# Stacking the queries by DMA from the sync queue instead of by selection products, with eight key buffers

## The reference, cut to what matters

```python
q = shape(H @ Wq, Lq) * dph ** (-0.5)        # H = layernorm(x), 16 heads of dph = 8
k = shape(T @ Wk, Lkv)                       # T = ctx_1024, 64 keys a batch
v = shape(T @ Wv, Lkv)
scores = jnp.einsum('bhqd,bhkd->bhqk', q, k) + ext        # ext masks keys
attn = jax.nn.softmax(scores.astype(jnp.float32), axis=-1)
x = x + jnp.einsum('bhqk,bhkd->bhqd', attn, v).transpose(0, 2, 1, 3).reshape(B, Lq, INNER) @ Wo
x = x + moe(layernorm(x))     # top 2 of 8 experts, a capacity per expert, silu(gate) * up, then wo
```

## Time and profile before

| what | value |
|---|---|
| median of 3 runs | 417.09 us (416.58 to 418.83) |
| the profiled execution | 418.15 us |
| its span, first to last instruction | 416.3 us |
| around the span | 1.85 us |
| mean granted clock of TensorE | 0.946 of full speed |
| busy over the span | PE 87%, DVE 63%, POOL 55%, ACT 46% |

### The profile page before, as it was taken

One profiled execution on the slowest core, in us unless ns is written; L12 is line 12 of the kernel. 1 busy time (PEld: TensorE's weight loads), 2 busy tenths in 40 slices (PEclk: granted clock), 3 DMA queues, 4 the chain that ended last, 5 costly groups with the idle time before them and its releaser, 6 DMA issues.

```text
span 416.3 us, 8894 instructions
## 1 busy us (share of the span) xinstructions
PE 360.4 (87%) x3012; PEld 311.7 (75%) x3012; DVE 260.7 (63%) x893; ACT 189.4 (46%) x430; POOL 228.9 (55%) x190
## 2 busy tenths in 40 slices
PE   0768889999899998849599999999999999999980
PEld 0456666677667665436599998999989899998980
DVE  4956888988998988762155455555554646455430
ACT  2444656667667765421233343434434444343320
POOL 9514231045437667777036566474764738557564
PEclk9986899999999999668699999999999999999996
DMA  8998011122223221111503724537363463723222
GB/s 246 262 308 291 3 21 31 30 46 67 41 47 90 64 81 56 65 58 54 136 9 32 168 27 73 114 33 168 27 119 73 35 156 32 157 35 34 26 27 25
DMA packets 41958, 35.05 MB, mean 84 GB/s; under 512 B 9136, under 2 KB 38320, under 8 KB 41776
## 3 DMA queue, kind: packets, MB, share of 16 engines
q1 hardware_dynamic: 27824, 24.72, 21.3%
q0 software_dynamic: 13568, 9.58, 17.0%
q10 hardware_dynamic: 528, 0.27, 0.2%
HBM read 21.64 MB, written 17.73 MB: 95 GB/s over the span
## 4 chain that ended last, share of the span: by engine, by line
PE 51%; DVE 19%; POOL 11%; issue 8%; DMA 6%; ACT 3%; POOLq 1%; DVEq 0%; ACTq 0%
PE bank L823 13%; PE bank L629 7%; PE bank L631 6%; POOL slots L443 6%; PE bank L630 6%; POOL out L477 4%; DMA out<-ys,idx 4%; PE bank L706 3%; DVE mneg L924 2%; PE bank L658 2%; PE bank L685 2%; DVE rall L1043 2%; PE bank L672 2%; PE bank L686 1%; PE bank L793 1%
## 5 line engine op out<-in xcount | busy, mean ns | idle before, releaser
L477 POOL DMA_INDIRECT out<-ys,idx x80 | 125.1, 1564 | 87.7 <-DVE ys L1122 36.9
L1148 DVE TENSOR_TENSOR h<-sg,bank 128x256 f32<-128x256 f32 x160 | 66.2, 418 | 77.4 <-ACT sg L614 70.2
L614 ACT ACTIVATE sg<-bank 128x256 f32<-128x256 f32 x160 | 61.5, 385 | 102.6 <-PE bank L631 96.2
L629 PE MATMUL bank<-ex_hi,w_hi 128*128 128x256 f32 x320 | 94.1, 294 | 4.1 <-DVE h L1148 4.1
L631 PE MATMUL bank<-ex_lo,w_hi 128*128 128x256 f32 x320 | 89.6, 280 | 0.0
L630 PE MATMUL bank<-ex_hi,w_lo 128*128 128x256 f32 x320 | 89.5, 280 | 0.0
L823 PE MATMUL bank<-w_raw,h 128*128 128x128 f32 x640 | 78.7, 276 | 1.7 <-DVE h L1148 1.4
L823 PEld LDWEIGHTS bank<-w_raw,h 128*128 128x128 f32 x640 | 74.7, 191 | 3.6 <-DVE h L1148 1.9
L443 POOL DMA_INDIRECT slots<-rall,slot x64 | 64.4, 1007 | 19.6 <-issue 15.5
L629 PEld LDWEIGHTS bank<-ex_hi,w_hi 128*128 128x128 f32 x320 | 61.1, 191 | 5.6 <-DVE h L1148 5.5
L630 PEld LDWEIGHTS bank<-ex_hi,w_lo 128*128 128x128 f32 x320 | 61.2, 191 | 0.0
(11 more groups left out here) (120 smaller groups left out, 540.2 us busy)
## 6 DMA issues: line engine op xcount, KB each, us to landing
slots<-in_empty SPq DMA_DIRECT2D x8, 660.0 KB, 11.0
xl<-slots SPq DMA_DIRECT2D x7, 660.0 KB, 6.7
w_raw<-in_wgu SPq DMA_DIRECT2D x8, 512.0 KB, 3.6
X<-in_x SPq DMA_DIRECT2D x4, 512.0 KB, 8.1
w_raw<-in_wdn SPq DMA_DIRECT2D x8, 256.0 KB, 4.0
out<-X SPq DMA_DIRECT2D x16, 128.0 KB
out<-ys,idx POOLq DMA_INDIRECT x80, 3.3
ks<-kc SPq DMA_DIRECT2D x72, 16.0 KB
```

The source lines that it names most:

```text
L477: nc.gpsimd.indirect_dma_start(out=out[:, :], out_offset=bass.IndirectOffsetOnAxis(ap=IDX[v][:, j:j + 1], axis=0), in_=YS[c][:, t, :], in_ ...
L614: nc.scalar.activation(SG[m % 2][:], GATE_PS[m % 2][:, 0:2 * P], ACT.Silu).then_inc(sg_ready, 1)
L629: nc.tensor.matmul(ps, hi, m_hi, start=True, stop=False)
L1148: nc.vector.tensor_tensor(H[n % 2][:, f, :], SG[m % 2][:], UP_PS[m % 2][:, 0:2 * P], ALU.mult).then_inc(h_ready, 1)
```

## The change

The queries of a batch are stacked by three DMAs on SP, one for each of the high, low, high parts; the eight products, their two copies and the selection matrices go. The columns of `Wq` are reordered on the host so that one DMA can write 32 rows and four groups from the 128 rows of `Q_HI` or `Q_LO`. There are eight key buffers: POOL spreads the keys of batches 0 to 7, and SP places those of batches 8 to 15 four batches at a time, a quarter of their rows in each of four steps. To make room, three arrays of the set-up share memory with arrays of the steps.

```diff
-KBUF = 4
+KBUF = 8
@@ set-up arrays
-        CTXM = s1("ctxm", [P, B, LK])
-        CTX_HI = s1("ctx_hi", [P, B * LK], F32R)
-        CTX_LO = s1("ctx_lo", [P, B * LK], F32R)
-        MASKI = s1("maski", [P, B, LK], I32)
-        SEL_HI = s1("sel_hi", [P, GROUPS, 3, 32], F32R)
-        SEL_LO = s1("sel_lo", [P, GROUPS, 3, 32], F32R)
+        CTX_HI, CTX_LO = [KS[:, 4 + n].rearrange("p g n -> p (g n)") for n in range(2)]
+        CTXM = PROBS[0][:, 0:2].rearrange("p g s q -> p (g s q)").rearrange("p (b k) -> p b k", k=LK)
+        MASKI = PROBS[1][:, 0:2].rearrange("p g s q -> p (g s q)").bitcast(I32)
@@ sync, after the fills, the weights, and its waits for k_used and ext_in
-            def place_keys(j):
-                b = slice(2 * j, 2 * j + 2)
-                to = slice(2 * j % KBUF, 2 * j % KBUF + 2)
-                done = keys_in[j % 2]
-                sp.wait_ge(st_full, 4 * (2 * j - 2))
-                for part in range(4):
-                    for h in range(HG):
-                        rows = slice(32 * part + DPH * h, 32 * part + DPH * h + DPH) if part < 3 else slice(ONE_ROW, ONE_ROW + 1)
-                        sp.dma_start(KS[rows, to, :, h * LK:(h + 1) * LK].bitcast(F32), KC[rows, b, :, :]).then_inc(done, 16)
+            def stack_queries(i):
+
+                sp.wait_ge(qlo_ready, i + 1)
+                if i >= 2:
+                    sp.wait_ge(st_full, 4 * (i - 1))
+                for part, q in enumerate((Q_HI, Q_LO, Q_HI)):
+                    sp.dma_start(QS[i % 2][32 * part:32 * part + 32, :, :].bitcast(F32),
+                                 q[:].bitcast(F32)).then_inc(qs_in[i % 2], 16)
+
+            def place_keys(i):
+
+                j, n = i // 4, i % 4
+                b, to = slice(4 * j, 4 * j + 4), slice(4 * j % KBUF, 4 * j % KBUF + 4)
+                done = keys_in[j % 2]
+                if n == 0:
+                    sp.wait_ge(st_full, 4 * (4 * j - 4))
+                for h in range(HG):
+                    rows = slice(32 * n + DPH * h, 32 * n + DPH * h + DPH) if n < 3 else slice(ONE_ROW, ONE_ROW + 1)
+                    sp.dma_start(KS[rows, to, :, h * LK:(h + 1) * LK].bitcast(F32), KC[rows, b, :, :]).then_inc(done, 16)
-            for j in range(2, B // 2):
-                place_keys(j)
-                store_sums(2 * j - 4)
-                store_sums(2 * j - 3)
-            for i in range(B - 4, B):
+            for i in range(B):
+                stack_queries(i)
+                if 5 <= i < 13:
+                    place_keys(i + 3)
+                if i >= 3:
+                    store_sums(i - 3)
+            for i in range(B - 3, B):
                 store_sums(i)
@@ gpsimd: the memsets and three copies that fill SEL_HI and SEL_LO are taken out
@@ scalar
-            def stack_queries(it, off, h):
-
-                i, u = 2 * it + off, off % 2
-                act.wait_ge(sel_full, 2 * i + (3 + h))
-                if h == 0:
-                    wait(act, st_full, 4 * i)
-                nc.scalar.copy(QS[1 - u][0:96, 2 * h:2 * h + 2, :].rearrange("p g q -> p (g q)"), QP[0:96, :]).then_inc(qs_ready, 1)
@@ scalar, step
                 if has(it, off, 1):
                     act.wait_ge(q_full, i + 2)
+                    wait(act, qs_in[u], 48 * ((i + 2) // 2))
                     nc.scalar.mul(Q_HI[:], M0[:, 0:LQ], SCALE).then_inc(qhi_ready, 1)
-                if has(it, off, 1):
-                    stack_queries(it, off, 0)
                     act.wait_ge(mt_full, i + 1)
+                    wait(act, st_full, 4 * (i - 1))
-                if has(it, off, 1):
-                    stack_queries(it, off, 1)
@@ tensor
                 if m == 0:
-                    pe.wait_ge(qs_ready, 2 * i + 2)
+                    pe.wait_ge(qs_in[u], 48 * (i // 2 + 1))
                     if i < KBUF:
                         pe.wait_ge(ks_ready, i + 1)
                     else:
-                        pe.wait_ge(keys_in[i // 2 % 2], PLACED * (i // 4))
+                        pe.wait_ge(keys_in[i // 4 % 2], PLACED)
-            def select(it, off, h):
-                i = 2 * it + off
-                if h == 0:
-                    pe.wait_ge(qlo_ready, i + 2)
-                wait(pe, qs_ready, 2 * i + (2 + h))
-                for gg in range(2):
-                    g = 2 * h + gg
-                    ps = QP[0:96, gg * LQ:(gg + 1) * LQ]
-                    nc.tensor.matmul(ps, SEL_HI[:, g].rearrange("p a c -> p (a c)"), Q_HI[:], start=True, stop=False)
-                    mm = nc.tensor.matmul(ps, SEL_LO[:, g].rearrange("p a c -> p (a c)"), Q_LO[:], start=False, stop=True)
-                mm.then_inc(sel_full, 1)
@@ tensor, step: both calls of select are taken out (between TX2 and the values; between the logits and L793)
@@ vector, step
-                    wait(dve, sel_full, 2 * i + 2)
+                    wait(dve, qs_in[u], 48 * ((i + 2) // 2))
@@ host
-        "wq": a["L0_xattn_Wq"],
+        "wq": np.ascontiguousarray(a["L0_xattn_Wq"].reshape(D, GROUPS, 32).transpose(0, 2, 1).reshape(D, D)),
```

More of the change, by code:

```diff
@@ L219, in program @@
         q_full, qhi_ready, qlo_ready = sem("q_full"), sem("qhi_ready"), sem("qlo_ready")
-        sel_full, qs_ready = sem("sel_full"), sem("qs_ready")
+        qs_in = [sem(f"qs_in{v}") for v in range(2)]
         ks_ready, v2_clear = sem("ks_ready"), sem("v2_clear")
@@ L299, in _ @@
         def _(sp):
-            sp.dma_start(MASKI[:].rearrange("p b k -> p (b k)"),
+            sp.dma_start(MASKI,
                          mask.rearrange("b k -> (b k)").rearrange("(a n) -> a n", a=1).to_broadcast([P, B * LK])
@@ L387, in _ @@
                 nc.gpsimd.memset(MNEG[v][:], 1.0)
-            nc.gpsimd.memset(RALL[:, :, D:ROW], 0.0)
+            nc.gpsimd.memset(RALL[:, :, D:ROW], 0.0).then_inc(pool_setup, 1)
             nc.gpsimd.memset(V2[:], 0.0).then_inc(v2_clear, 1)
-            nc.gpsimd.memset(SEL_HI[:, :, 1, :].bitcast(F32), 0.0)
-            nc.gpsimd.memset(SEL_LO[:].bitcast(F32), 0.0).then_inc(pool_setup, 1)
             pool.wait_ge(pool_setup, 3)
             pool.wait_ge(const_in, 16)
[L395 to L398, removed]
             nc.gpsimd.tensor_copy(TRI[:], C[:, C_TRI:C_TRI + P])
@@ L491, in _ @@
             act.wait_ge(setup, 3)
-            nc.scalar.copy(CTX_HI[:], CTXM[:].rearrange("p b k -> p (b k)")).then_inc(ctx_split, 1)
+            nc.scalar.copy(CTX_HI, CTXM.rearrange("p b k -> p (b k)")).then_inc(ctx_split, 1)
             for n in range(8):
@@ L642, in _ @@
             pe.wait_ge(k_used, 8)
-            pe.wait_ge(pool_setup, 5)
+            pe.wait_ge(pool_setup, 4)
             def row_scores(it, off, m):
@@ L767, in step @@
                     rank(ROUTED[off])
-                if has(it, off, 1):
-                    select(it, off, 0)
                 if has(it, off, -1):
@@ L784, in step @@
                     mm.then_inc(lg_full, 1)
-                if has(it, off, 1):
-                    select(it, off, 1)
                 if has(it, off, -1):
@@ L861, in _ @@
             dve.wait_ge(mask_in, 16)
-            nc.vector.tensor_copy(MASKF[:], MASKI[:]).then_inc(setup, 1)
+            nc.vector.tensor_copy(MASKF[:], MASKI.rearrange("p (b k) -> p b k", k=LK)).then_inc(setup, 1)
             dve.wait_ge(setup, 1)
@@ L868, in _ @@
             any_b = ANY[:].unsqueeze(2).to_broadcast([P, B, LK])
-            nc.vector.tensor_tensor(CTXM[:], CTX[:], any_b, ALU.mult).then_inc(setup, 1)
+            nc.vector.tensor_tensor(CTXM, CTX[:], any_b, ALU.mult).then_inc(setup, 1)
             dve.wait_ge(wsplit, 1)
@@ L872, in _ @@
             dve.wait_ge(ctx_split, 1)
-            nc.vector.tensor_tensor(CTX_LO[:], CTXM[:].rearrange("p b k -> p (b k)"), CTX_HI[:].bitcast(F32), ALU.subtract
+            nc.vector.tensor_tensor(CTX_LO, CTXM.rearrange("p b k -> p (b k)"), CTX_HI.bitcast(F32), ALU.subtract
                                     ).then_inc(ctx_split, 1)
@@ L903, in _ @@
                 nc.vector.tensor_tensor(lo.bitcast(F32R), K_PS[n % 4][64:96, :].rearrange("p (b k) -> p b k", k=LK), lo, ALU.subtract).then_inc(k_used, 1)
-            dve.wait_ge(pool_setup, 5)
+            dve.wait_ge(pool_setup, 4)
             def norm(i, v):
```

## The result

The changed kernel takes 439.37 us (median of 4 runs, 436.71 to 439.75) against 417.96 us of the kernel before in the same job (416.58 to 420.37): a ratio of 1.0487, interval 1.0451 to 1.0523. The forecast was 432.4 us. The measured time lies in the range from 421 to 441 that was stated for it together with its rivals, but above the forecast's own range of 427 to 438. The profiled span is 437.4 us, 21.1 more.

The account below looks back on a forecast made before the run. DVE was taken to set the pace in the steps. Start 11.7, first steps -1.2, later steps -0.8, spreadings 3.4, keys 2.2 make 15.3 us more: 432.4 us, own range 427 to 438, with rivals 421 to 441.

Parts of the forecast that it names:

- The first stack: Start: batch 0's stack lands behind fills and weights in SP's queue, row scores 11.7 us late.
- The first rival: Start: the stack is not held by the fills and lands at 33.0, 0.4 late; 421.1 us, chance 0.09.
- The spreadings: Steps 3 to 6: four more key spreadings on POOL hold up DVE's RALL, 3.4 us in all.
- The last quarter of the keys: Batches 8 and 12: the last key copies land after the row scores could start; 1.1 us each, 2.2 together.
- The first steps: Steps 0 and 1, at low clock: dropped products save PE time, 1.2 us gained.
- The later steps: Seven undisturbed steps at full clock: each gains about 0.11 us, 0.8 us together.
- The later stacks: Each later step: a stack takes 4.0 us from Q_LO, covered by 4.6 to 4.7 us of step; no cost.
- The second rival: All steps: every stack is late, 5.3 us or more from Q_LO; 438.4 us, chance 0.12.
- The sum: Whole kernel: all terms together add 15.3 us, giving 432.4 us.
- a clock below full speed in the steps: Steps: sign of a wrong prediction, if with PE less busy it shows as longer projections on DVE's path.
- the fourth rival: POOL's sends: they run at their own pace from an earlier start and swallow the delay; 417 us, chance 0.03.

Follow-up runs that it names:

- experiment 1: Changed kernel with the stacks of batches 0 and 1 issued from ACT's queue instead of SP's: 440.19 us, 1.0523 to the kernel before.
- experiment 2: Changed kernel with slot fills, zeros and expert weights issued on SP behind later stacks: 428.07 us, 1.0212 to the kernel before.
- Experiment 5: Changed kernel with POOL's key spreadings moved early, four ahead of batch 0 and four in its first step: 436.09 us, 1.0388.
- Experiment 6: Kernel before with only the eight key buffers, their spreadings and quarters added; selecting products and copies kept: 422.97 us, 1.0102.
- experiment 3: Changed kernel with SP issuing each quarter of the keys ahead of the stack of its turn: 436.66 us, 1.0426.
- experiment 4: Changed kernel with products of no use on PE ahead of the row scores of batches 0, 8 and 12: 435.57 us, 1.0426.
- experiment 9: Changed kernel with fills and weights later, Q_HI copies first, non-waiting key quarters ahead of stacks, spreadings one, four, three: 420.70 us, 1.0061.

## Why the prediction was right, and where it was off

**The first stack: right in size (11.1 against 11.7), its mechanism too narrow.** The prediction had it that "the queue delivers in about the order of issue". The changed kernel fits that: the stack lands about with the last weights. But experiment 1 takes the stack out of that queue and gains only 1.6 us; experiment 2 takes away the bulk transfers and gains nearly all. The load on the engines is enough to hold it, and moving it to another queue is no cure. The first rival, which priced a stack that isn't held, got its lateness about right for a start without fills (34.19 against 33.0).

**The spreadings: right.** Steps 3 to 6 slip by 3.05 us; forecast were 3.4 less 0.33 for three quicker steps. RALL took 1.59, 1.58, 1.12 and 1.59 us. Experiment 5 gives 3.8 back over steps 2 to 6. Experiment 6 loses 4.07 in steps 3 to 6, but its clock was at 0.50 from 52 to 62 us, into step 3.

**The last quarter of the keys: mis-sized.** Forecast 2.2 us, measured 6.1 (3.24 and 2.89). The wait was somewhat above its forecast of 1.1 each, 1.6 and 1.8 us (the gains of experiment 3 less those of experiment 4), within the bounds. But the step priced a wait of PE at its own length. Behind it the granted clock stood at 0.50 for over 5 us, and that cost 1.6 and 1.1 us more.

**The first steps: of the wrong sign.** Forecast -1.2 us, measured +1.7. The saved products were costed at a low clock that was taken to be the same in both kernels. From the first row scores to X of step 2 it was 0.65 in the mean, against 0.81 before, and at 0.88 in experiment 4 the stretch took 1.6 us less. The other 1.3 us aren't settled: in experiment 4 the two steps take 27.35 us, no less than the 27.23 before, though at a higher clock, so the saving itself doesn't show there.

**The later steps: right.** Undisturbed ones take 7.83 us in place of 7.94 (step 7), the 0.11 forecast. Eight products and two copies a step were worth that much. Steps 9 to 11 won another 0.12 us. Steps 13 to 16 lost 1.07, of which 0.74 was made up by the last send; neither is explained.

**The later stacks: right.** From issue to landing 3.2 us as the median of the 28 later copies of `Q_HI`, and PE's waits for a stack, in 32 to 190 (total us, times, longest):

```profile
qs<-q_hi SPq DMA_DIRECT2D x28, 128.0 KB, 3.2
```

```profile
PE bank L651 <- DMA qs<-q_hi: 14.2, 2, 13.9
```

Nearly all of it is the first. One of the others, its last issue and the row scores that use it:

```profile
77.59 0.60 SPq L332 DMA_DIRECT2D qs<-q_hi  x1
```

```profile
81.83 0.48 PE L651 MATMUL bank<-ks,qs 97*128 97x256 f32 x2
```

`Q_LO` ended at 76.30, so the stack, 3.2 us after that issue, is there 4.5 us later, and the row scores start 5.5 later: hidden. In a step without a spreading the cover is 4.7, with little to spare. The second rival falls with it. Its 438.4 us came nearer to the measured time than the forecast's 432.4, but by luck: behind the first, PE's waits for a stack came to 0.3 us in all.

**The sum.** 11.1 + 1.7 + 3.05 + 6.1 and small change make 22.1 us at the last send, of which 21.1 reach the end; the forecast's 15.3 lacked 3.9 at the keys and 2.9 at the first steps. Of these, 2.8 and 1.6 went when experiment 4 raised the clock. The forecast had no term for that; it named a clock below full speed in the steps among the signs that it is wrong, and this sign appeared. That the delay reaches the end, against the fourth rival, is seen in the sends.

No version beat the kernel before. The best, experiment 9, is 0.6% slower, with its steps as long as before; what it loses, it loses ahead of X of step 1.

## What to carry to other kernels

Price a wait of TensorE by the wait and by the slower stretch behind it: at batches 8 and 12 waits of 1.6 and 1.8 us cost 3.2 and 2.9. Here a small DMA that the path needs was late while bulk transfers ran, whichever queue issued it; look at moving the bulk, not the small one. When work is removed from engines that don't set the pace, its gain is only what the pace-setting engine waited for (0.11 us a step here), and each thing that was moved to pay for it has a price of its own.

## What was not expected of the hardware

- After two waits of 1.27 and 1.62 us the granted clock was 0.50 over the 5.3 and 5.8 us that followed, with PE busy throughout; with products in the waits it stayed at 1.00.
- A stack of 0.39 MB on a queue of its own moved nothing for 4.6 us and then packet for packet with the other queue's bulk (320 against 326 in 4 us), so that the row scores started 13.5 us after `Q_LO`, against 15.1 on the queue of the bulk.
- A copy of 113 rows ran at 26 GB/s, one engine's worth, and SP's next issue took 20.85 us.
- Spreadings on GpSimd stretched RALL, XN and RNEG, VectorE operations that work on SBUF alone, by 0.5 to 3.4 us. Those that read a bank of PSUM (the maxima, XT_LO, `Q_LO`, ERR) stayed as they were, and so did the small searches of the routing (FIND_INDEX8, 0.15 us), which work on SBUF too.
